# Sum stage of an eight-layer graph network: index copies and per-buffer waits on GpSimd, ten first columns per load, selections four tiles ahead

## What is computed

```
h = features
for each layer (W, b, g, beta):
    h   = h * norm_out
    agg = segment_sum(h[src], dst) * norm_in
    h   = gelu(layer_norm(agg @ W + b) * g + beta)
out = layernorm(x + h)
```

## Time and profile before

| what | us |
|---|---|
| median of three runs (1677.46 to 1686.68) | 1680.89 |
| the profiled execution, its own time | 1669.91 |
| its span, from first to last instruction | 1668.2 |
| eight sum stages, first matmul to last column addition | 612.0 |
| PE busy in them | 407.2 |
| mean granted clock of PE in the span | 0.808 |

### The profile page before, as it was taken

How to read it: one execution, slowest core, us unless ns; L and a number is a source line. 1 busy time by engine, 2 the same in 40 slices (tenths; PEclk the granted TensorE clock), 3 DMA queues, 4 the chain that set the end, 5 groups by cost and what they waited for, 6 DMA issues and landing times.

```text
span 1668.2 us, 29286 instructions
## 1 busy us (share of the span) xinstructions
PE 1110.4 (67%) x6235; PEld 916.9 (55%) x6235; DVE 880.2 (53%) x2153; ACT 528.1 (32%) x853; POOL 846.9 (51%) x1023
## 2 busy tenths in 40 slices
PE   7665378677596695776776696679956769992000
PEld 7444123666575575656656585667846667882000
DVE  6445577245354372463563274326733226776776
ACT  4132230232332332233333232333323333441444
POOL 1554300545445464455455365445745445765886
PEclk9556559788898897798898898789987889996555
DMA  0930000523514415225225324441244448545998
GB/s 14 377 130 3 2 1 6 159 82 126 158 57 139 133 69 170 78 107 163 71 106 164 107 76 138 139 126 66 91 139 147 149 126 321 189 169 180 312 302 291
DMA packets 98038, 224.52 MB, mean 135 GB/s; under 512 B 14496, under 2 KB 14496, under 8 KB 97968
## 3 DMA queue, kind: packets, MB, share of 16 engines
q0 software_dynamic: 34432, 104.72, 21.2%
q1 hardware_dynamic: 57200, 107.52, 17.9%
q10 hardware_dynamic: 6336, 11.54, 1.9%
HBM read 137.91 MB, written 85.82 MB: 134 GB/s over the span
## 4 chain that ended last, share of the span: by engine, by line
PE 53%; issue 12%; DMA 10%; DVE 8%; POOL 5%; ACT 4%; another core or an unknown queue 3%; ACTq 2%; DVEq 2%; POOLq 0%; SPq 0%
PE ps_a L1200 16%; PE ps_y L1220 9%; PE ps_y L1221 9%; PE ps_y L1225 9%; DMA rows<-h_rows,slot 4%; POOL rows L507 3%; DMA rows<-h_rows,idx_f 2%; PE ps_y L1216 2%; DMA h_rows<-rows 2%; PE ps_a L1115 2%; DVE agg_t L607 2%; PE ps_a L1181 1%; ACT agg_t L958 1%; DVEq L821 1%
## 5 line engine op out<-in xcount | busy, mean ns | idle before, releaser
L1200 PE MATMUL ps_a<-sel,rows 128*128 128x128 f32 x2560 | 407.0, 323 | 278.1 <-DVE sel L789 122.8
L1200 PEld LDWEIGHTS ps_a<-sel,rows 128*128 128x128 f32 x2560 | 377.1, 233 | 309.6 <-issue 309.0
L456 POOL DMA_INDIRECT rows<-h_rows,slot x290 | 279.8, 965 | 258.3 <-issue 124.6
L995 ACT ACTIVATE agg_t<-ps_a 128x508 f32 x320 | 190.7, 596 | 520.7 <-PE ps_a L1200 369.8
L464 POOL TENSOR_TENSOR s_lo<-agg_t,s_hi 128x512 fp32r<-128x512 f32 x168 | 216.9, 1293 | 251.3 <-ACT s_hi L1000 251.3
L789 DVE TENSOR_SCALAR sel<-iota,by_tile 128x128 f32<-128x128 f32 x344 | 126.0, 370 | 395.6 <-PE ps_a L1200 207.2
L1220 PE MATMUL ps_y<-w_hi,s_hi 128*128 128x512 f32 x672 | 268.5, 400 | 10.9 <-ACT s_hi L1000 10.8
L1221 PE MATMUL ps_y<-w_lo,s_hi 128*128 128x512 f32 x672 | 267.6, 398 | 0.0
L1225 PE MATMUL ps_y<-w_hi,s_lo 128*128 128x512 f32 x672 | 183.5, 396 | 0.0
L862 DVE BATCH_NORM_STATS2 small<-ps_y 128x6 f32<-128x512 f32 x168 | 117.3, 698 | 96.1 <-PE ps_y L1225 95.9
L1220 PEld LDWEIGHTS ps_y<-w_hi,s_hi 128*128 128x128 f32 x672 | 129.0, 192 | 42.0 <-issue 15.1
(11 more groups left out here) (210 smaller groups left out, 1268.2 us busy)
## 6 DMA issues: line engine op xcount, KB each, us to landing
h_rows<-rows SPq DMA_DIRECT2D x124, 256.0 KB, 2.0
h_rows<-agg_t SPq DMA_DIRECT2D x1, 20480.0 KB
out<-agg_t SPq DMA_DIRECT2D x78, 256.0 KB
agg_t<-in_x SPq DMA_DIRECT2D x19, 1024.0 KB, 5.7
h_rows<-rows ACTq DMA_DIRECT2D x44, 256.0 KB, 2.3
w_raw<-in_Ws SPq DMA_DIRECT2D x32, 256.0 KB
rows<-h_rows,slot POOLq DMA_INDIRECT x290
rows<-in_ln_g SPq DMA_DIRECT2D x8, 256.0 KB, 3.8
```

The source lines that it names most:

```text
L456: g.indirect_dma_start(out=rows[:, k, :], out_offset=None, in_=table[:, :], in_offset=bass.IndirectOffsetOnAxis(ap=slot[:, k:k + 1], axis=0))\
L995: a.activation(agg_t[:, :, bass.ds(r0 + 1, P - 1)], ps_a[k % GS][:, :, 1:P], ACT.Copy)\
L1200: m = mm(ps_a[k % GS][:, b, :], rows[:, k, b * P:(b + 1) * P], sel[:, k % GS, :], start=True, stop=True)
```

## The change

Five edits, all in the sum stage:

1. The copies of row numbers into `slot` move from DVE to POOL. POOL issues each before the fifth gather of a half, for the other half; the first two are issued ahead of layer 0, and the first half of the next layer's at a layer's end.
2. Each gather now waits for its own buffer (`agg_ok` of the tile ten before), and for the landing of the gather five before it (`g_in`), instead of one wait for five gathers. Each of these waits is followed by a semaphore increment (`tick`), as elsewhere. Layer 0's first group is written out ahead of the loop.
3. DVE and ACT load the ten `r0` of a group with one instruction at the group's start, instead of one load for each tile.
4. Selections are made four tiles ahead (`AHEAD = 4`), and in a tile's turn they come behind the column addition instead of ahead of it. Their wait on `agg_ok` is gone; the wait on `ev_ok` before the addition covers it.
5. `PRIME`, the offset that all counting semaphores start from, goes from 8 to 10.

```
-AHEAD = 3
+AHEAD = 4
...
+        def first_columns(engine, t):
+            return nc.values_load_multi_w_load_instructions(q0[0:1, bass.ds(t, UN)], engines=(engine,),
+                                                            min_val=0, max_val=N + 1)[1]
...
+            def indices(L, t, half):
+                table = idx_h if L > 0 else idx_now
+                g.tensor_copy(slot[:, half * GS:half * GS + GS], table[:, bass.ds(t, GS)]).then_inc(ix_ok, 1)
+            def turn(L, table, ib, group):
+                first = L == 0 and isinstance(group, int)
+                for k in range(UN):
+                    half, n = k // GS, ib * 2 + group * 2
+                    if k % GS == 0:
+                        pool.wait_ge(ix_ok, n + (L + half + 1))
+                        pool.sem_inc(tick, 1)
+                    if half == 1 or not first:
+                        pool.wait_ge(g_in[(k + GS) % UN], (ib + group + half) * 16)
+                        pool.sem_inc(tick, 1)
+                        if k % GS == GS - 1:
+                            indices(L, group * UN + (half + 1) * GS, 1 - half)
+                    pool.wait_ge(agg_ok, done(ib * UN + group * UN + (k - UN + 1)))
+                    pool.sem_inc(tick, 1)
+                    g.indirect_dma_start(out=rows[:, k, :], ...).then_inc(g_in[k], 16)
...
-                    for k in range(UN):
-                        if k % GS == 0:
-                            pool.wait_ge(ix_ok, ib * 2 + group * 2 + (L * 2 + k // GS + 1))
-                            pool.sem_inc(tick, 1)
-                            pool.wait_ge(agg_ok, done(i + k - GS))
-                            pool.sem_inc(tick, 1)
...
+                        firsts = first_columns(mybir.EngineType.DVE, t)
                         for k in range(UN):
-                            r0 = dve.value_load(q0[0:1, bass.ds(t + k, 1)], min_val=0, max_val=N + 1)
-                            dve.wait_ge(agg_ok, done(i + k + 1))
-                            select(t + k + AHEAD, k + AHEAD)
                             dve.wait_ge(edge_ok, done(i + k))
                             dve.sem_inc(dve_tick, 1)
                             dve.wait_ge(ev_ok, done(i + k + 1))
-                            col = agg_t[:, :, bass.ds(r0, 1)]
+                            col = agg_t[:, :, bass.ds(firsts[k], 1)]
                             v.tensor_tensor(col, ps_a[k % GS][:, :, 0:1], col, ALU.add).then_inc(edge_ok, 1)
-                            if k % GS == GS - 1:
-                                indices(L, t + k // GS * GS + UN, k // GS)
+                            select(t + k + AHEAD, k + AHEAD)
...
+                    firsts = first_columns(mybir.EngineType.Activation, t)
                     for k in range(UN):
-                        r0 = act.value_load(q0[0:1, bass.ds(t + k, 1)], min_val=0, max_val=N + 1)
```

More of the change, by code:

```diff
@@ L23 @@
 ITS_MIN, PAIRS_MIN = 3, 3
-PRIME = 8
+PRIME = 10
 CT = 8
@@ L445, in _ @@
             pool.wait_ge(setup_ok, 1)
-            def sum_stage(L, table, its, ib):
-                with pool.Fori(0, its) as group:
-                    i = ib * UN + group * UN
-                    for k in range(UN):
-                        if k % GS == 0:
-                            pool.wait_ge(ix_ok, ib * 2 + group * 2 + (L * 2 + k // GS + 1))
-                            pool.sem_inc(tick, 1)
-                            pool.wait_ge(agg_ok, done(i + k - GS))
-                            pool.sem_inc(tick, 1)
-                        g.indirect_dma_start(out=rows[:, k, :], out_offset=None, in_=table[:, :],
-                                             in_offset=bass.IndirectOffsetOnAxis(ap=slot[:, k:k + 1], axis=0))\
-                         .then_inc(g_in[k], 16)
+            def indices(L, t, half):
+                table = idx_h if L > 0 else idx_now
+                g.tensor_copy(slot[:, half * GS:half * GS + GS], table[:, bass.ds(t, GS)]).then_inc(ix_ok, 1)
@@ new lines, in turn @@
+            def turn(L, table, ib, group):
[12 more added lines that the diff above has]
+                    pool.sem_inc(tick, 1)
+                    g.indirect_dma_start(out=rows[:, k, :], out_offset=None, in_=table[:, :],
+                                         in_offset=bass.IndirectOffsetOnAxis(ap=slot[:, k:k + 1], axis=0))\
+                     .then_inc(g_in[k], 16)
@@ L460, in low @@
+            def sum_stage(L, table, its, ib):
+                if L == 0:
+                    turn(0, table, 0, 0)
+                with pool.Fori(1 if L == 0 else 0, its) as group:
+                    turn(L, table, ib, group)
+                if L + 1 < LAYERS:
+                    pool.wait_ge(ix_ok, ib * 2 + its * 2 + (L + 1))
+                    pool.sem_inc(tick, 1)
+                    indices(L + 1, 0, 0)
             def low(j, c, k):
@@ L490, in stored @@
                     pool.sem_inc(tick, 1)
+            for half in range(2):
+                indices(0, half * GS, half)
             counts = layer_counts(pool, 0)
@@ L790, in select, with first_tiles @@
                                 ALU.is_equal, ALU.mult).then_inc(sel_ok, 1)
[L792 to L800, removed]
+            def first_tiles():
                 for k in range(AHEAD):
@@ L853, in sum_stage @@
                 if L + 1 < LAYERS:
-                    dve.wait_ge(ix_ok, ib * 2 + its * 2 + (L * 2 + 2))
                     dve.wait_ge(sel_ok, ib * UN + its * UN + (L + 1) * AHEAD)
                     dve.sem_inc(dve_tick, 1)
-                    first_tiles(L + 1)
+                    first_tiles()
             def centre(j, k):
@@ L895, in _ @@
             link(v.memset(agg_t[:, :, 1:4 * P], 0.0))
-            first_tiles(0)
+            first_tiles()
             counts = layer_counts(dve, 0)
@@ L989, in sum_stage @@
                     t = group * UN
+                    firsts = first_columns(mybir.EngineType.Activation, t)
                     for k in range(UN):
                         i = ib * UN + t
-                        r0 = act.value_load(q0[0:1, bass.ds(t + k, 1)], min_val=0, max_val=N + 1)
                         hold(agg_ok, done(i + k + 1))
                         hold(ev_ok, done(i + k))
-                        a.activation(agg_t[:, :, bass.ds(r0 + 1, P - 1)], ps_a[k % GS][:, :, 1:P], ACT.Copy)\
+                        a.activation(agg_t[:, :, bass.ds(firsts[k] + 1, P - 1)], ps_a[k % GS][:, :, 1:P], ACT.Copy)\
                          .then_inc(ev_ok, 1)
```

## The result

The changed kernel takes 1716.40 us (median, 1714.67 to 1717.36) against 1683.27 us for the kernel before with the runs made beside it: ratio 1.0199, 95% interval 1.0166 to 1.0232. It is 33 us slower; the forecast was 27 us faster, and the range ended at 1702. Ratios and medians here are of undisturbed executions only; that leaves out two of one kernel's ten (edits 1, 2 and 5, late), which took 1876 and 3520 us.

A forecast was written before the change was run, and what follows sets the result against it. Waits between engines were taken to bound the kernel, with 204.8 us of PE idle in the sum stages. Terms -18 - 29 + 14 - 9 + 15 = -27 us gave 1654 us from 1680.9; 8-in-10 range 1605 to 1702.

The forecast's parts named there:

- The reading of the bound: Sum stages: 204.8 us of PE idle time to win; selection waits 122.8 us, landing waits within the stages some 24.
- Term C: Group heads on DVE: 3.1 us each, delaying PE 0.8 us at 16 places and 0.2 at eight; +14 us.
- rival of dear heads: Group heads on DVE: ten registers cost ten loads, 2.9 us more each, two thirds exposed, +47: 1701 us; chance 17%.
- Term D: Sum stage's end: last addition comes 0.2 to 0.3 us after last copy, 1.1 us in eight layers; -9 us.
- A: POOL's gathers in the sum stages: data runs ahead, so 18 of 24 us of landing waits go; -18 us.
- B: Selections four ahead: one more tile in stock takes 29 of 65 us of short waits; -29, between 0 and -60.
- E: Spread-out gathers: more tiles end beside a gather, up to one more hold of 3.79 us in each layer; +15 us.
- held signals set the pace: Rival, sum stages: late signals go only when POOL pauses, still 1.8 us a tile, no change: 1681 us; chance 16%.
- POOL falls behind: Rival, gathers on POOL: new waits don't hide below a gather, 1.8 us a tile, +10: 1691 us; chance 10%.
- wrong, if the head is over 4.3 us: Sign for DVE's group head in the profile after: 3 to 3.5 us expected, over 4.3 us would show the forecast wrong.

The follow-up runs named there:

- edits 1, 2 and 5, late: Kernel before with only POOL's index copies, per-buffer gather waits and PRIME changed, in a late-signal job: 1660.6 us against 1668.9, ratio 0.9944.
- prompt job: Job where at most three of 320 tiles have PE's signal over 0.5 us behind the recorded end; the kernel before takes 1519 us.
- prompt pair: Changed kernel and the same with edit 3 undone, in one prompt job: 1583.7 and 1509.5 us, 1.0404 and 0.9941 of the kernel before.
- kernel with loads for each tile: Changed kernel with edit 3 alone undone: 0.9911 and 0.9941 of the kernel before in prompt jobs, 0.9884 (1660.2 us) in a late-signal job.
- late-signal job: Job where over a hundred of 320 tiles have PE's signal over 0.5 us behind the recorded end; the kernel before takes 1669 to 1684 us.

## Why the prediction was wrong

**The reading of the bound** held. Selections and landings were what PE waited for, and the 24 us of landings inside the stages went. What taking a wait away is worth did not follow from its size: the other kind grew in its place.

**Term C, the head (+14), is the step that failed.** Edit 3 costs 50 to 53 us in this company where the forecast had +14. Three faults:
- *Its size.* I had one load and twenty steps at 3.1 us; measured 3.8 to 4.4 in even groups and 5.1 to 5.6 in odd ones. The twenty steps were right (2.77 us). The load wasn't: I took 0.30 us, that of one register, because the order of instructions has one TENSOR_LOAD there. The bound from above, ten loads, gave 6.0. The Trainium skill, "Runtime: NRT & Kernel Launch", section "Instruction fetch mechanics", has about 200 ns for each register even in bulk; it doesn't say there whether that holds for loads from SBUF, as these are. The trace shows 1.07 us in even groups, 0.09 us for each further register, half of that, and 2.30 us in odd ones, 0.22 each, a little over it. The sign that this would turn the sum was in the text (1.1 us dearer than 3.1; the mean of the 24 is 4.71, 1.6 dearer), as the rival of dear heads, given 17%.
- *Its place.* I compared one moment: tile 24's selection at 1275.16 before and 1276.4 after, 0.5 to 1.1 us. In the trace that selection comes 5.10 us behind the split's start, which is 1277.7 in the time of before, and PE starts tile 24 2.1 us later than it did then (1276.29), not 0.5 to 1.1. At the 8 plain heads I wrote 0.2 us, since DVE had gained. PE's wait ahead of the fifth tile is 4.2 to 6.4 us there in the last layer. The stock of selections can't be built up, however fast DVE is between heads: tile k + 4 is selected only when tile k has come through PE, ACT and the addition. When DVE's load begins at these eight heads, PE has one or two tiles left, 1.2 to 1.4 us of work; in the prompt job three, 1.9 us. At the other 16 it has next to nothing left, or in the prompt job at most 2.3 us. What a head lasts beyond that is lost.
- *The second engine.* ACT has the same head, and I costed DVE's alone. ACT's by itself costs 28 us.

And there was no term for PE's clock after a long wait: by place it is 30 of 83 us in the prompt pair, and 5 of some 62 with late signals.

**Term D, last tiles (-9),** is right in its rows and worth nothing. The end of layer 0's sum stage, beside the earlier trace rows:

```profile
360.63 0.60 ACT L1012 ACTIVATE agg_t<-ps_a 128x508 f32 x1 [0.30 <-PE ps_a L1217]
...
361.36 0.17 DVE L847 TENSOR_TENSOR agg_t<-ps_a,agg_t 128x4 f32 x1 [0.37 <-ACT agg_t L1012]
```

The addition ends 0.30 us behind the last copy, 1.38 before. But from PE's last product of that stage to the last of the W stage it is 46.7 us before (352.0 to 398.8) and 46.9 after (360.3 to 407.2). The next stage doesn't start by that addition, as I had it: PE's first product of the W stage even begins 0.5 us ahead of it in the kernel with loads for each tile (late-signal job).

**Terms A, B and E (-18, -29, +15: -32)** are all but edit 3, and gave -21 us in the late-signal job. A with its share of E gave 9 alone, B 3, all together 21. The three come from different jobs and their intervals are wide (3 to 15 us for the 9), but the waits say the same: each edit alone lengthens the waits that the other would take away. E was seen and its place wrong: not a hold more in every run of spread gathers but one longer hold at the start of each layer, 27 us for my 15.

By these three: C 39 us too low, D 9, the rest 11, together 59 of the 60 us between -27 and +33. They close by construction, since C's price is the measured total less the rest; its place and size rest on the waits and the heads above.

**The rivals.** That held signals set the pace, with no change in time, is out: with the signals prompt the change is slower still. That POOL falls behind is out: its group now reads

```profile
L472 POOL DMA_INDIRECT rows<-h_rows,slot x290 | 281.6, 971 | 241.4 <-issue 114.6 <-PE ps_a L1217 100.2 <-remote 23.9
```

with 971 ns for a gather as against 965 in the earlier trace rows, and 0.30 us from one to the next where no buffer is awaited. Dear heads were the case that came, 1701 us forecast and 1716 measured, and its condition, heads more than 1.1 us dearer than 3.1, was met. Of my own signs, "wrong, if the head is over 4.3 us" is met in all odd groups and one even one.

## What to carry to other kernels

Work that is put together at the head of a loop must be costed as one lump against the stock that the consumer has at that moment, and a ring whose slots come free only through the whole chain may never have its full depth in stock; at the heads here, three tiles of four at most. Ten small loads between waits were 50 to 74 us cheaper than the same work in one piece, though DVE is busy for less time with the latter. If two engines have the same head, cost both. Add what a long wait costs in PE's clock. And where an operation is larger than any that the rows show, its price from the smallest form is a lower bound and not the likely value.

## What the runs showed of the hardware

- A register load of ten words takes 1.07 to 1.2 us (DVE) or 1.00 (ACT) where its start within `q0` is a multiple of 48 or of 80 bytes, and 2.30 or 2.2 at odd multiples of 40; a load of one word takes 0.30 (DVE). One change of layout took 22 us off the kernel.
- After a long wait PE works at the lower level of its clock for a tile and more: 2.05 us for a tile of eight records, against 1.13, after 22 of 24 waits of 5.7 us. In the prompt pair that is 30 of the 83 us that the heads cost from first to last product.
- The same kernel takes 1519 us in some jobs and 1669 to 1684 in others. The gathers take 0.95 us and come every 1.25 us in both, where no buffer is awaited. The difference is in the sum stages: 617 us where the kernel before was traced with late signals, against 473 and 602 for the kernel with loads for each tile in a prompt and a late-signal job. At a prompt layer's start the copies follow PE at once:

```profile
1167.55 8.64 PE L1217 MATMUL ps_a<-sel,rows 128*128 128x128 f32 x52 [11.46 <-DMA rows<-h_rows,slot]
...
1171.55 0.60 ACT L1012 ACTIVATE agg_t<-ps_a 128x508 f32 x1 [1.02 <-PE ps_a L1217]
...
1172.44 0.60 ACT L1012 ACTIVATE agg_t<-ps_a 128x508 f32 x1 [0.29 <-PE ps_a L1217]
```

  Here six tiles are summed without a break, beside the same gathers; the signal of tile 2 comes 0.01 us behind its recorded end, and in the late-signal traces of the same kernel 7 to 9 us. What holds the signals elsewhere stays open.
